# A pipelined kernel of four graph layers: the loop over passes written out, two biases added on VectorE, the scores spread with one fp32 matmul, other orders

## The chip, the cores and the metric

One core of a Trainium2 chip. The metric is the device time of one execution in microseconds: the median of several runs. A core has TensorE (PE in the profile; its weight loads are PEld), VectorE (DVE), ScalarE (ACT), GpSimd (POOL) and SyncE (SP), each with an instruction queue of its own that runs strictly in the order written, and they meet only at semaphores.

## What is computed

The input is 128 small graphs: `x` (128 graphs, 128 nodes, 256 features) and a weighted adjacency matrix `adj` (128x128 for each graph). Each of four layers takes `h = max(layernorm(x), 0)` and adds its own result to `x`:

```
L0  hypergraph convolution: with H = (adj != 0) and degrees from H and adj's first row,
    twice  out = Dn * (H @ (Be * (H^T @ (x @ W^T)))) + b, with relu and a layernorm between
L1  tanh(norm(adj) @ h @ W + b)
L2  s = h @ w @ a;  A = exp(leaky(8*tanh((s_i + s_j)/8))) * adj, rows rescaled;  A @ h @ w
L3  three times  adj @ (h @ W) + b, with relu after the first and the second
```

Everything is in float32. The kernel must keep near to fp32 precision, which shapes the way it multiplies.

## The kernel before

**Tiling.** Two graphs (J = 2) are worked on together as one unit, with the 128 nodes on the partitions. Four such units, the streams A to D, are in flight at a time, a quarter of a period apart; 16 passes of four streams make the 128 graphs. This text calls the work of one stream in one pass a turn: there are 64 turns, and in the steady state PE works in each turn on parts of all four streams.

**Steps.** A turn has seven products by a matrix of graph size (steps 0U to 6U) and seven by weights (0W to 6W). A U step is four fp32 matmuls of 128 columns into a PSUM bank (1U: eight). ScalarE then copies the bank into an fp32r tile UHI (`take`, L442), VectorE writes the rest, bank minus UHI, into ULO (`low`, L590), and the W step (`weigh`, L346) multiplies in three parts, UHI by WLO, UHI by WHI and ULO by WHI, as fp32r matmuls of 256 columns (512 for 0W). WHI and WLO are the weights split in the same way in the start. The trace records an fp32 matmul as two rows, an fp32r matmul as one.

**Biases of 4W and 5W.** The first matmul of these two steps (L357, L358) multiplies a constant tile SHARES by BIAS, 128x512 in fp32r, which puts the bias into the bank. BIAS holds the fp32r half of the bias on 64 partitions and the remainder on the others; it is made in the start by four casts (L535) and four subtractions (L541). When the step has ended, ScalarE takes the relu straight from the bank (`relu`, L483) and frees it; the next U step (5U or 6U) waits for this relu.

**Scores.** In layer L2 VectorE sums the score of each node (2N, L629). Two small operations split it, a cast SHI (2H, L637) and a difference SLO (2L, L641). PE spreads the scores over the columns (3S, `spread_scores`, L379) with four fp32r matmuls of 128 columns, each with one column of scores as stationary operand, repeated 128 times, and the identity as moving one. ScalarE's tanh and two exps, and VectorE's 3L and 3R, follow; `sums_done` at the end of 3R frees that bank.

**Banks.** U steps other than 1U, W steps other than 0W, G and 3S share four single banks in turn, so each waits for the fourth user before it to be released (`bank_free`, L292); 0W and 1U share two double banks.

**Order.** What each engine does next is written out by hand. Five tables of slots (L20 to L37) give each step of stream A a time within a period of 88; stream B's are 22 later, and so on. `ordered` (L40) sorts them. The slots do nothing but give the order in which each engine's instructions are written. `run` (L162) writes the pass 0, then a hardware loop (`Fori`, L173) over passes 1 to 15, whose waits compare with register values, then what is left of the last pass. SyncE has its own loop (L265).

Of the kernel before, what the change touches and what calls it, by code (L numbers as in the profile page):

```python
# [37 lines left out]


def ordered(slots):  # L40

# [8 lines left out]
PE_ORDER, ACT_ORDER, DVE_ORDER, POOL_ORDER, SP_ORDER = map(ordered, (PE_SLOTS, ACT_SLOTS, DVE_SLOTS, POOL_SLOTS, SP_SLOTS))  # L50


def program(nc, xs, adj_t, adj_r, w1t, w2t, l1w, l2w, l2wt, l3w1, l3w2, l3w3, cols, b1, b2, l1b, l3b1, l3b2, l3b3, out):
# [6 lines left out]
    with ExitStack() as ctx:  # L60
# [76 lines left out]
        WIDE_TURNS = [x for x in PE_ORDER if x[1] in WIDE_STEPS]  # L137
        BANK_TURNS = [x for x in PE_ORDER if x[1] not in WIDE_STEPS]

        def bank(s, step):  # L140
            turns, banks = (WIDE_TURNS, WIDE) if step in WIDE_STEPS else (BANK_TURNS, BANK)
            return banks[[x[:2] for x in turns].index((s, step)) % len(banks)]

        SETUP = WIDE[1 - [x[:2] for x in WIDE_TURNS].index(("A", "0W")) % 2]

# [14 lines left out]
        LIVE = [(s, back) for s in STREAMS for back in (0, -1)]  # L160

        def run(eng, order, parts, setup={}, per_pass=(1,)):  # L162

            def values(k):
                return {(s, back): dict(dma=16 * (k + back + 1), v=[J * done_at(s, k + back) - J + j + 1 for j in range(J)],
                                        **{f"n{m}": m * done_at(s, k + back) for m in per_pass}) for s, back in LIVE}

            for s, step, back in order:
                if not back:
                    parts[step](s, values(0)[s, 0], 0)  # L170
                    if (s, step) in setup:
                        setup[s, step]()
            with eng.Fori(1, GROUPS) as k:  # L173
                loop = {(s, back): {f"n{m}": eng.snap(len(STREAMS) * m * k + m * done_at(s, back)) for m in per_pass}
                        for s, back in LIVE}
                dma = {back: eng.snap(16 * k + 16 * (back + 1)) for back in (0, -1)}
                for s, back in LIVE:
                    loop[s, back]["dma"] = dma[back]
                    loop[s, back]["v"] = [eng.snap(len(STREAMS) * J * k + J * done_at(s, back) - J + j + 1) for j in range(J)]
                for s, step, back in order:  # L180
                    parts[step](s, loop[s, back], loop)
            for s, step, back in order:
                if back:
                    parts[step](s, values(GROUPS)[s, back], GROUPS)

        @block.sync
        def _(sp):
# [65 lines left out]
            def one_pass(k):  # L253
                for s, step, back in SP_ORDER:
                    if isinstance(k, int) and not (0 if step == "O" else 1) <= k + back < GROUPS:
                        continue
# [16 lines left out]
        def _(pe):  # L273
# [18 lines left out]
            def bank_free(s, step, k):  # L292
# [543 lines left out]
```

## Time and profile before

| | |
|---|---|
| median of 3 runs | 1413.41 us (1413.35 to 1413.74) |
| the profiled execution, its own time | 1413.38 us |
| its span in the trace | 1411.6 us (1.8 us lie around it) |
| TensorE busy | 1373.7 us, 97% |
| VectorE busy | 1168.9 us, 83% |
| ScalarE busy | 999.3 us, 71% |
| GpSimd busy | 998.7 us, 71% |

How to read it: a busy time is the union of the times of an engine's instructions. Matmuls overlap in the records, so what one costs is read as the distance between the starts of two that follow each other, in the timeline, not as its recorded length. Instructions that only wait, branch or set registers are not counted as busy. In rows that name a group, x is how many records it has.

### The profile page before, as it was taken

Reading aid. Unit: us, or ns where it says so; the run is one execution under the profiler, and the core shown is the slowest. Engines: PE = TensorE matmul, PEld = TensorE weight load, DVE = VectorE, ACT = ScalarE, POOL = GpSimd, SP = SyncE. Lnnn points to the kernel's source line nnn. Section 1 sums busy time; section 2 is a strip of 40 time slices with the busy share of each in tenths; the row PEclk is TensorE's granted clock in tenths of the full one; section 3 lists DMA queues with packets and bytes.
Section 4 is the critical chain, followed back from the end, with each engine's and each line's share of the span. In section 5 each row is a group of like instructions: output and inputs, shape, how many; then the busy total and the mean of one; then the engine's idle time right before and its main releaser. Section 6 shows DMA issues by size and latency. Waiting matters only on the chain.

```text
span 1411.6 us, 34650 instructions
## 1 busy us (share of the span) xinstructions
PE 1373.7 (97%) x10900; PEld 1325.3 (94%) x10900; DVE 1168.9 (83%) x3873; ACT 999.3 (71%) x2376; POOL 998.7 (71%) x2005
## 2 busy tenths in 40 slices
PE   4899999999999999999999999999999999999997
PEld 3799999999999999999999999999999999999996
DVE  5788888888888888888888888888888888888874
ACT  3577777777777777777777777777777777777763
POOL 3677777777777777777777777777777777777751
PEclk8999999999999999999999999999999999999999
DMA  7011120110110110110110110121211111111100
GB/s 190 1 42 28 53 52 26 52 52 26 52 52 26 52 52 26 52 52 26 52 52 26 52 52 27 52 52 28 50 52 29 49 52 29 49 52 32 31 20 23
DMA packets 83080, 62.70 MB, mean 44 GB/s; under 512 B 40305, under 2 KB 65521, under 8 KB 83057
## 3 DMA queue, kind: packets, MB, share of 16 engines
q1 hardware_dynamic: 83056, 62.43, 16.2%
q8 instruction: 11, 0.18, 0.1%
q14 instruction: 13, 0.10, 0.0%
HBM read 45.62 MB, written 16.78 MB: 44 GB/s over the span
## 4 chain that ended last, share of the span: by engine, by line
PE 95%; DVE 2%; POOL 1%; ACT 1%; issue 0%; DMA 0%; SPq 0%; DVEq 0%; POOLq 0%; ACTq 0%
PE BANK L366 29%; PE BANK L331 24%; PE BANK L373 15%; PE WIDE L366 8%; PE WIDE L342 8%; PE WIDE L373 4%; PE BANK L358 2%; PE BANK L316 2%; PE BANK L385 2%; DMA W<-in_w1t 0%; PE WIDE L279 0%; DVE BN_A L552 0%; POOL LN_A L730 0%; DVE WLO1W L502 0%; DVE BN_C L552 0%
## 5 line engine op out<-in xcount | busy, mean ns | idle before, releaser
L445 ACT ACTIVATE UHI_B<-BANK 128x512 fp32r<-128x512 f32 x96 | 57.3, 597 | 45.1 <-PE BANK L331 45.1
L445 ACT ACTIVATE UHI_C<-BANK 128x512 fp32r<-128x512 f32 x96 | 57.2, 596 | 42.2 <-PE BANK L331 42.2
L445 ACT ACTIVATE UHI_D<-BANK 128x512 fp32r<-128x512 f32 x96 | 57.2, 596 | 41.0 <-PE BANK L331 41.0
L445 ACT ACTIVATE UHI_A<-BANK 128x512 fp32r<-128x512 f32 x96 | 57.2, 596 | 40.2 <-PE BANK L331 40.2
L593 DVE TENSOR_TENSOR ULO_D<-BANK,UHI_D 128x512 fp32r<-128x512 f32 x96 | 65.9, 686 | 23.1 <-ACT UHI_D L445 22.4
L593 DVE TENSOR_TENSOR ULO_C<-BANK,UHI_C 128x512 fp32r<-128x512 f32 x96 | 65.9, 686 | 17.2 <-ACT UHI_C L445 16.5
L593 DVE TENSOR_TENSOR ULO_A<-BANK,UHI_A 128x512 fp32r<-128x512 f32 x96 | 65.9, 687 | 15.3 <-ACT UHI_A L445 15.0
L593 DVE TENSOR_TENSOR ULO_B<-BANK,UHI_B 128x512 fp32r<-128x512 f32 x96 | 65.8, 686 | 13.6 <-ACT UHI_B L445 12.9
L726 POOL TENSOR_TENSOR LN_D<-MV_D,EPS 128x2 f32<-128x2 f32 x80 | 15.7, 196 | 75.9 <-DVE MV_D L560 75.9
L726 POOL TENSOR_TENSOR LN_A<-MV_A,EPS 128x2 f32<-128x2 f32 x80 | 15.8, 197 | 73.1 <-DVE MV_A L560 73.1
L726 POOL TENSOR_TENSOR LN_B<-MV_B,EPS 128x2 f32<-128x2 f32 x80 | 15.9, 198 | 64.3 <-DVE MV_B L560 64.3
L726 POOL TENSOR_TENSOR LN_C<-MV_C,EPS 128x2 f32<-128x2 f32 x80 | 15.7, 196 | 61.9 <-DVE MV_C L560 61.8
L730 POOL TENSOR_TENSOR LN_B<-LN_B,MHALF 128x2 f32<-128x2 f32 x80 | 55.9, 699 | 1.3
L730 POOL TENSOR_TENSOR LN_D<-LN_D,MHALF 128x2 f32<-128x2 f32 x80 | 55.8, 697 | 1.3
L730 POOL TENSOR_TENSOR LN_A<-LN_A,MHALF 128x2 f32<-128x2 f32 x80 | 55.7, 697 | 1.3
L730 POOL TENSOR_TENSOR LN_C<-LN_C,MHALF 128x2 f32<-128x2 f32 x80 | 55.7, 696 | 1.3
L414 ACT ACTIVATE H_A<-RES_A,LN_A 128x256 f32<-128x256 f32 x96 | 52.2, 594 | 2.0 <-POOL LN_A L738 2.0
L331 PE MATMUL BANK<-T_D,H_D 128*128 128x128 f32 x384 | 52.0, 278 | 1.6 <-ACT H_D L486 1.4
L414 ACT ACTIVATE H_D<-RES_D,LN_D 128x256 f32<-128x256 f32 x96 | 52.2, 594 | 1.9 <-POOL LN_D L738 1.9
L414 ACT ACTIVATE H_C<-RES_C,LN_C 128x256 f32<-128x256 f32 x96 | 52.2, 594 | 0.9 <-POOL LN_C L738 0.9
L331 PE MATMUL BANK<-T_C,H_C 128*128 128x128 f32 x384 | 51.9, 278 | 0.9 <-ACT H_C L486 0.7
L414 ACT ACTIVATE H_B<-RES_B,LN_B 128x256 f32<-128x256 f32 x96 | 52.2, 595 | 0.5 <-POOL LN_B L738 0.5
(508 smaller groups left out, 5920.1 us busy)
## 6 DMA issues: line engine op xcount, KB each, us to landing
X_A<-in_xs SPq DMA_DIRECT2D x16, 256.0 KB, 2.8
X_B<-in_xs SPq DMA_DIRECT2D x16, 256.0 KB, 2.8
X_C<-in_xs SPq DMA_DIRECT2D x16, 256.0 KB, 2.8
X_D<-in_xs SPq DMA_DIRECT2D x16, 256.0 KB, 2.8
out_rows<-O_A SPq DMA_DIRECT2D x16, 256.0 KB, 2.0
out_rows<-O_B SPq DMA_DIRECT2D x16, 256.0 KB, 2.1
out_rows<-O_C SPq DMA_DIRECT2D x16, 256.0 KB, 2.1
out_rows<-O_D SPq DMA_DIRECT2D x16, 256.0 KB, 2.1
```

What stands on the lines that cost most here:

```text
L316: last = nc.tensor.matmul(bank(s, "G")[:, j * (P + 2):(j + 1) * (P + 2)], HT[s][:, j, :], BHT[s][:, j, :], start=True, stop=True)
L331: last = nc.tensor.matmul(bank(s, step)[:, at:at + P], lhs[s][:, j, m * P:(m + 1) * P], rhs(s, j), start=True, stop=True)
L342: last = nc.tensor.matmul(bank(s, "1U")[:, j, m * P:(m + 1) * P], Z[s][:, j, m * P:(m + 1) * P], GZ[s][:, j, :], start=True, stop=True)
L358: nc.tensor.matmul(to[:, :], SHARES[:, :], BIAS[step][:, :, :], start=True, stop=False)
L366: nc.tensor.matmul(dst, UHI[s][:, at[m]:at[m] + P], w[:, m, :], start=(w is lo and m == 0 and not biased), stop=False)
L373: last = nc.tensor.matmul(dst, ULO[s][:, at[m]:at[m] + P], hi[:, m, :], start=False, stop=(m == chunks - 1 and (j == J - 1 or not biased)))
L385: last = nc.tensor.matmul(bank(s, "3S")[:, j * P:(j + 1) * P], part[s][:, j:j + 1].to_broadcast([P, P]), IDENTR[:, :], start=(part is SHI) ...
L414: nc.scalar.activation(dst[s][:, j, :], src[s][:, j, :], ACT.Relu, bias=LN[s][:, NB, j:j + 1], scale=LN[s][:, RSTD, j:j + 1]).then_inc(sem ...
L445: nc.scalar.activation(UHI[s][:, 0:J * D], bank(s, step)[:, :], ACT.Copy).then_inc(sem(f"c{step}"), 1)
L593: nc.vector.tensor_tensor(ULO[s][:, 0:J * D], bank(s, step)[:, :], UHI[s][:, 0:J * D].bitcast(F32), ALU.subtract).then_inc(sem(f"l{step}"), 1)
L726: nc.gpsimd.tensor_tensor(ve, MV[s][:, :, 1], EPS[:, :], ALU.add).then_inc(sem("ve" + tag), 1)
L730: nc.gpsimd.tensor_tensor(rstd, ve, MHALF[:, :], ALU.pow)\
```

## The change

- The hardware loops are gone: every engine's 16 passes are written out one after the other, and each wait has a constant. The rotation of the banks is worked out over all passes.
- 4W and 5W have no bias matmul. A new VectorE step of each name adds the bias row to the bank (128x512, `b4W`, `b5W`) and writes H; ScalarE's relu then waits for that step, reads H and writes H. The bank is released by VectorE's step. BIAS, SHARES and their eight operations in the start are gone.
- 3S has two fp32 matmuls, straight from the scores and the identity, in the place of four fp32r ones. VectorE's 2H and 2L are gone, with the tiles SHI, SLO and IDENTR.
- All five slot tables have other values. In a turn PE's order was 5U 3U 2W 5W G 3W 1U 6U 1W 6W 0U 4U 3S 0W 4W 2U. It is now 5U 2U 3U 5W 2W 3W G 6U 1U 6W 1W 4U 0U 3S 4W 0W (each step of whichever stream is due). On VectorE 4W now stands right ahead of 3L, 3R and 3E, and 5W behind 2U, 0A and 3U.

```diff
 PE_SLOTS = {
-    "G": 5.35, "0U": 12.31, "0W": 15.06, "1U": 28.24, "1W": 29.30, "2U": 37.53, "2W": 47.58, "3S": 58.05,
-    "3U": 67.04, "3W": 71.77, "4U": 79.22, "4W": 81.45, "5U": 88.19, "5W": 92.43, "6U": 94.56, "6W": 97.75}
+    "G": 5.03, "0U": 18.28, "0W": 23.04, "1U": 29.55, "1W": 34.98, "2U": 45.66, "2W": 48.39, "3S": 63.29,
+    "3U": 68.21, "3W": 70.61, "4U": 83.87, "4W": 86.20, "5U": 89.28, "5W": 91.09, "6U": 93.96, "6W": 100.54}
...
 DVE_SLOTS = {
+    "T": 3.90, "X": 4.63, "XA": 14.25, "DA": 18.63, "DB": 18.99, "DC": 20.57, "DD": 30.10, "0U": 32.13,
+    "0W": 35.26, "0S": 36.47, "0A": 37.90, "1U": 42.66, "1W": 49.42, "1S": 50.94, "1A": 52.77, "2U": 59.47,
+    "2W": 61.69, "2S": 64.38, "2A": 64.62, "2N": 71.31, "3L": 77.37, "3R": 78.92, "3E": 79.04, "3U": 82.01,
+    "3I": 83.33, "3J": 84.12, "3W": 84.15, "3S": 84.54, "3A": 84.64, "4U": 94.08, "4W": 98.78, "5U": 102.44,
+    "5W": 104.12, "6U": 107.62, "6W": 109.61}
...
-        def run(eng, order, parts, setup={}, per_pass=(1,)):
...
-            with eng.Fori(1, GROUPS) as k:
...
+        def run(slots, parts, setup={}, per_pass=(1,)):
+
+            for s, step, k in ordered(slots, GROUPS):
+                parts[step](s, passed(s, k, per_pass), k)
+                if not k and (s, step) in setup:
+                    setup[s, step]()
...
-                    if biased:
-                        nc.tensor.matmul(to[:, :], SHARES[:, :], BIAS[step][:, :, :], start=True, stop=False)
...
-                pe.wait_ge(sem("scores_split"), c["n1"])
+                pe.wait_ge(sem("s_ready"), c["n1"])
                 bank_free(s, "3S", k)
                 for j in range(J):
-                    for part in (SHI, SLO):
-                        last = nc.tensor.matmul(bank(s, "3S")[:, j * P:(j + 1) * P], part[s][:, j:j + 1].to_broadcast([P, P]),
-                                                IDENTR[:, :], start=(part is SHI), stop=(part is SLO))
+                    last = nc.tensor.matmul(bank(s, "3S", k)[:, j * P:(j + 1) * P], ST[s][:, SC, j:j + 1].to_broadcast([P, P]),
+                                            IDENT[:, :], start=True, stop=True)
...
             def relu(step):
                 def f(s, c, k):
-                    act.wait_ge(sem(f"p{step}"), c["n1"])
-                    nc.scalar.activation(H[s][:, :, :], bank(s, step)[:, :], ACT.Relu).then_inc(sem(f"c{step}"), 1)
+                    act.wait_ge(sem(f"b{step}"), c["n1"])
+                    nc.scalar.activation(H[s][:, :, :], H[s][:, :, :], ACT.Relu).then_inc(sem(f"c{step}"), 1)
...
+            def biased(step):
+                def f(s, c, k):
+                    dve.wait_ge(sem(f"p{step}"), c["n1"])
+                    rows = bank(s, step, k)[:, :].rearrange("p (j d) -> p j d", j=J)
+                    nc.vector.tensor_tensor(H[s][:, :, :], rows, pair(BIAS[step][:, :]), ALU.add).then_inc(sem(f"b{step}"), 1)
```

## Rows read from the trace of the kernel before

**Rows 1.** The page: busy times, granted clock, the chain by engine.

```profile
PE 1373.7 (97%) x10900; PEld 1325.3 (94%) x10900; DVE 1168.9 (83%) x3873; ACT 999.3 (71%) x2376; POOL 998.7 (71%) x2005
...
PEclk8999999999999999999999999999999999999999
...
PE 95%; DVE 2%; POOL 1%; ACT 1%; issue 0%; DMA 0%; SPq 0%; DVEq 0%; POOLq 0%; ACTq 0%
```

**Rows 2.** Busy times from 76 to 1357 us, then in two stretches of one loop turn.

```profile
core 0: us, PE busy (x) PEld busy (x) DVE busy (x) ACT busy (x) POOL busy (x), PEclk, DMA share, GB/s
...
76.00:1357.00 1281.00, 1280.96 (x10286) 1242.17 (x10285) 1089.68 (x3627) 938.22 (x2243) 940.82 (x1874) 1.00 0.15 42
...
97.00:181.60 84.60, 84.60 (x682) 82.07 (x681) 72.01 (x241) 61.95 (x148) 62.19 (x124) 1.00 0.17 45
520.00:604.60 84.60, 84.60 (x682) 82.07 (x681) 72.04 (x241) 61.96 (x148) 62.20 (x124) 1.00 0.15 43
```

**Rows 3.** A wait of PE in the start: us in total, times, longest.

```profile
PE WIDE L342 <- ACT GZ_A L461: 4.0, 1, 4.0
```

**Rows 4.** Timeline of PE, one stream's turn: start, us, then the group.

```profile
700.00 0.39 PE L358 MATMUL BANK<-BIAS5W,SHARES 128*128 128x512 f32 x1
700.23 0.40 PE L366 MATMUL BANK<-WLO5W,UHI_B 128*128 128x256 f32 x2
700.46 0.40 PE L366 MATMUL BANK<-WHI5W,UHI_B 128*128 128x256 f32 x2
...
702.01 0.49 PE L366 MATMUL BANK<-WLO3W,UHI_C 128*128 128x256 f32 x2
702.33 0.39 PE L366 MATMUL BANK<-WHI3W,UHI_C 128*128 128x256 f32 x2
...
703.47 1.95 PE L342 MATMUL WIDE<-GZ_A,Z_A 128*128 128x128 f32 x16
705.25 1.06 PE L331 MATMUL BANK<-T_B,H_B 128*128 128x128 f32 x8
...
711.28 1.06 PE L331 MATMUL BANK<-T_C,H_C 128*128 128x128 f32 x8
712.10 0.30 PE L385 MATMUL BANK<-IDENTR,SHI_D 128*128 128x128 f32 x1
...
712.58 0.68 PE L366 MATMUL WIDE<-WLO0W,UHI_B 128*128 128x512 f32 x2
...
721.15 0.39 PE L358 MATMUL BANK<-BIAS5W,SHARES 128*128 128x512 f32 x1
```

**Rows 5.** DVE and ACT groups of stream A, by form.

```profile
L593 DVE TENSOR_TENSOR ULO_A<-BANK,UHI_A 128x512 fp32r<-128x512 f32 x96 | 65.9, 687 | 15.3 <-ACT UHI_A L445 15.0
...
L639 DVE CAST SHI_A<-ST_A 128x2 fp32r<-128x2 f32 x16 | 11.5, 719 | 0.6
...
L643 DVE TENSOR_TENSOR SLO_A<-ST_A,SHI_A 128x2 fp32r<-128x2 f32 x16 | 2.4, 149 | 0.0
...
L486 ACT ACTIVATE H_A<-BANK 128x512 f32<-128x512 f32 x32 | 18.9, 591 | 12.3 <-PE BANK L373 12.3
```

**Rows 6.** The larger instruction queue, q8: 50 to 176 us, then 176 to 1360 us.

```profile
q8 instruction: 7, 0.11, 0.4%
...
q8 instruction: 1, 0.02, 0.0%
```

**Rows 7.** Timeline of the start: DVE, then PE.

```profile
26.88 0.48 DVE L535 CAST BIAS4W<-L3B 128x256 fp32r<-128x256 f32 x2
...
29.25 0.69 DVE L502 TENSOR_TENSOR WLO2W<-O_A,WHI2W 128x512 fp32r<-128x512 f32 x1
...
34.03 3.78 PE L342 MATMUL WIDE<-GZ_A,Z_A 128*128 128x128 f32 x16 [4.04 <-ACT GZ_A L461]
```

**Rows 8.** Timeline of the end, stream D alone: PE and ACT.

```profile
1399.33 0.60 ACT L486 ACTIVATE H_D<-BANK 128x512 f32<-128x512 f32 x1 [2.01 <-PE BANK L373]
...
1399.98 1.16 PE L331 MATMUL BANK<-T_D,H_D 128*128 128x128 f32 x8 [0.69 <-ACT H_D L486]
```

More of the change, by code:

```diff
@@ L82, in program @@
         B2, L1B, L3B1, L3B2, L3B3 = (sb(n, [P, D]) for n in ("B2", "L1B", "L3B1", "L3B2", "L3B3"))
-        BIAS = {step: sb(f"BIAS{step}", [P, J, D], F32R) for step in ("4W", "5W")}
-        SHARES = sb("SHARES", [P, P], F32R)
+        BIAS = {"4W": L3B1, "5W": L3B2}
         BW = sb("BW", [P, D])
@@ L89, in program @@
         IDENT = sb("IDENT", [P, P])
-        IDENTR = sb("IDENTR", [P, P], F32R)
         OFFDIAG = sb("OFFDIAG", [P, P])
@@ L136, in program, with banks_for, bank @@
         WIDE_STEPS = ("0W", "1U")
[L137 to L144, printed above, removed]
+        def banks_for(step):
+            return WIDE if step in WIDE_STEPS else BANK
+        TURN, LAST_USER, users = {}, {}, {True: [], False: []}
+        for user in ordered(PE_SLOTS, GROUPS):
+            alike, banks = users[user[1] in WIDE_STEPS], banks_for(user[1])
+            TURN[user] = len(alike) % len(banks)
+            if len(alike) >= len(banks):
+                LAST_USER[user] = alike[-len(banks)]
+            alike.append(user)
+        def bank(s, step, k):
+            return banks_for(step)[TURN[s, step, k]]
+        SETUP = WIDE[1 - TURN["A", "0W", 0]]
         W1, W2, W2G = sb("W1", [P, DC, DH]), sb("W2", [P, HC, D]), sb("W2G", [P, HC, D])
@@ L158, in done_at, with passed @@
             return len(STREAMS) * k + STREAMS.index(s) + 1
-        LIVE = [(s, back) for s in STREAMS for back in (0, -1)]
-        def run(eng, order, parts, setup={}, per_pass=(1,)):
[L164 to L172, printed above, removed]
-            with eng.Fori(1, GROUPS) as k:
[L174 to L184, printed above, removed]
+        def passed(s, k, per_pass=(1,)):
+            return dict(dma=16 * (k + 1), v=[J * done_at(s, k) - J + j + 1 for j in range(J)],
+                        **{f"n{m}": m * done_at(s, k) for m in per_pass})
+        def run(slots, parts, setup={}, per_pass=(1,)):
[3 more added lines that the diff above has]
+                    setup[s, step]()
         @block.sync
@@ L251, in _ @@
             parts = {"X": load_x, "F": load_front, "W": load_first_row, "D": load_diagonal, "R": load_r, "T": load_t, "O": store}
[L253 to L256, printed above, removed]
-                    before = back if step == "O" else back - 1
-                    n = len(STREAMS) * k + done_at(s, before)
-                    if isinstance(k, int):
-                        parts[step](s, k + back, n)
-                    else:
-                        parts[step](s, k + back, sp.snap(n))
-            one_pass(0)
-            with sp.Fori(1, GROUPS - 1) as k:
-                one_pass(k)
-            one_pass(GROUPS - 1)
-            one_pass(GROUPS)
+            for s, step, k in ordered(SP_SLOTS, GROUPS):
+                if k or step == "O":
+                    parts[step](s, k, done_at(s, k if step == "O" else k - 1))
             for s in STREAMS:
@@ L330, in f @@
                             at = j * D + m * P
-                            last = nc.tensor.matmul(bank(s, step)[:, at:at + P], lhs[s][:, j, m * P:(m + 1) * P], rhs(s, j),
+                            last = nc.tensor.matmul(bank(s, step, k)[:, at:at + P], lhs[s][:, j, m * P:(m + 1) * P], rhs(s, j),
                                                     start=True, stop=True)
@@ L366, in f @@
                                 nc.tensor.matmul(dst, UHI[s][:, at[m]:at[m] + P], w[:, m, :],
-                                                 start=(w is lo and m == 0 and not biased), stop=False)
+                                                 start=(w is lo and m == 0), stop=False)
                         if step == "1W":
```

112 lines of the change are left out of this document (38 added, 74 removed), and 11 rows, old and new, of tables (ACT_SLOTS, DVE_SLOTS).

## The prediction

> **What bounds the kernel now.** I read the page first: PE is busy for 97% of the span, its granted clock is full in all slices but the first, where it is 0.8, and the chain that ended last is PE for 95% [rows 1]. A busy PE need not be a full one, so I asked next for windows. From 76 to 1357 us PE is busy for 1280.96 of 1281.00 us [rows 2]: it waits for nothing. Two bias matmuls of the same step, one turn apart,, the first and the last row of [rows 4], start 21.15 us from each other, and 64 turns of that are 1354 us; the rest is the filling and emptying of the pipeline. In those 1281 us (60.6 turns) DVE is busy for 1089.7 us and ACT for 938.2 [rows 2], so 18.0 and 15.5 us of each turn. In the steady state only PE's own work counts; what the others do costs nothing while it comes in time. The reader should take from this that two questions decide: how much PE work goes, and whether PE still never waits.
>
> All sums are against the profiled execution, 1413.38 us (span 1411.6 and 1.8 around it); the median is 1413.41, so the two can be taken as one.
>
> **Bias matmuls.** The one of 5W starts at 700.00 and the next matmul at 700.23 [rows 4], so it holds PE for 0.23 us. There are two in each turn, 128 in all: 128 x 0.23 = **29.4 us less**. The Trainium skill (TensorE: Matmul & The Clock Gate, Back-to-back issue gap) states a sustained spacing of 131 ns for matmuls of 512 columns, and by that only 16.8 us would go. The trace has 230 ns for this one in its place, and the sum goes by it.
>
> **Scores.** Four fp32r matmuls from 712.10 to 712.58 take 0.48 us [rows 4]. The two fp32 matmuls in their place are four records of the kind of 1U, whose 16 records take 705.25 - 703.47 = 1.78 us, 0.111 each, so 0.445. A change from fp32 to fp32r costs something as well: the first WLO3W pair behind G takes 0.32 us where a pair of 5W takes 0.23 [rows 4]. The old order has four blocks of fp32 in a turn, the last of them leading into the cheap fp32r 3S; the new one has three. That would be 0.035 + 0.04 us less, 5 us in all. Against it: a T unit inside a block takes 0.82 us (711.28 to 712.10), 0.103 for a record, when it is followed by today's 3S, and the same eight records at 1U's 0.111 take 0.89; with 3S in fp32 this shorter unit may go. That is 0.07 us a turn, 5 us more. Stationary operands read with a repeat of one column are fp32r here, in fp32 no row shows them; between those ends I take **0**, range -5 to +5.
>
> **DVE.** It gains two adds of 128x512 from PSUM, like the ULO operation at 0.687 us, and loses the cast at 0.719 and the difference at 0.149 [rows 5]: 18.0 + 1.37 - 0.87 = 18.5 us in a turn. PE's new turn is 21.15 - 0.46 = 20.69, so DVE is at 89%, from 85%. ACT's relu (0.591 [rows 5]) stays, now with its input in SBUF: 15.5 of 20.7, 75%. GpSimd does the same as before. Their load costs **0**; what hides it is 2.2 us of free DVE time in a turn, down from 3.1, and the order has to keep each result in time.
>
> **The added step on the path.** 5U waits for 4W's relu and 6U for 5W's. In the end, where nothing hides it, relu starts at 1399.33 and 5U at 1399.98 [rows 8], 0.65 us; the add ahead of it is about 0.69 + 0.04, so the way from the end of a W step to its U step becomes some 1.42 us. What covers it in the steady state: behind 4W comes 0W, 12 matmuls of 512 at about 0.23, 2.8 us. Behind 5W come 2W and 3W (six pairs of 0.23 each) and G (four fp32 records of 0.111), 3.2 us. So 1.4 and 1.8 us are left for operations that stand ahead in DVE's and ACT's queues. Followed through one turn, DVE has 2U's ULO, a small aggregate and 3U's ULO in front of 5W's add (1.5 us), but these can start before 5W has ended, and I find 6U served about 0.4 us early. 2U's normalised input, 1U's scaled G (behind 5W's relu on ACT) and 6W's ULO come out 0.3 to 0.5 us early too. The margins are thin and all on the right side. The banks: the add releases 4W's, which 5W needs next, behind 0W, 5U, 2U and 3U, some 5.5 us; 5W's goes to 6U, which waits for 5W's relu in any case. Bank of 3S: 3U is still the fourth user, with 0W, 4W, 5U and 2U between (about 6 us, as before). Steady state: **0**.
>
> **Loops written out.** Each wait on a register becomes one on a constant, and no engine branches. PE is busy for 84.60 of 84.60 us in the stretch from 97 us and again in the one from 520 [rows 2]. Both hold a turn of the loop or its seam, so the branch cost PE no idle time; 0.04 us a pass, one unit of what I can read, is the most: **0.6 us less**. The price is more code to fetch. Queue q8 brought seven packets from 50 to 176 us and one from 176 to 1360 [rows 6]: the loop's code stayed where it was. Now the fetching of the first stretch goes on all the time, and in the first stretch PE was as full as later. Cost **0**. The Trainium skill (Runtime: NRT & Kernel Launch, Instruction fetch mechanics) has a taken branch wait for a fetch when its target is not in a small window; by that each of 14 turns back would have cost a fetch. The rows show no such gap.
>
> **Start.** The eight bias operations on DVE, from 26.88 to 29.25 us [rows 7], stand ahead of the aggregate that leads to GZ_A, for which PE waits 4.0 us at 34.03 [rows 3, 7]. With them gone that wait is **2.4 us** shorter. The first pass is otherwise in PE's old order. **End.** With one or two streams left the added step is bare: 4W to 5U for B, C and D, and 5W to 6U for D, 0.73 us each: **3 us more**.
>
> Sum: 1413.4 - 29.4 + 0 - 0.6 - 2.4 + 3.0 = **1384.0 us**, 2.1% less. What a measurement can tell from no change is about 0.2%, 2.8 us.
>
> **The rivals.**
> - *A partial stall (15%).* One of the thin margins is negative and PE waits some 0.3 us in each turn: 64 x 0.3 = 19, **1403 us**. For it: DVE at 89% with strict order, four margins of 0.3 to 0.5 us. Against: the load leaves 2.2 us.
> - *The add is late (7%), slower than before.* 5W's add stands behind an operation of DVE that itself waits for ACT (the statistics of 0W need its relu, in front of 2U's ULO), so that 6U waits for the add and one more operation: 0.69 + 0.59 = 1.3 us beyond the cover in each turn, minus the 0.46 gained: 64 x 0.8 = 54, **1467 us**. It decides from the point where PE waits over 0.46 us in a turn. Against it: the wait must outlast 3.2 us of PE work.
> - *Matmuls of another pace (8%).* The same matmuls stand at 0.22 to 0.24 us a pair here. If new neighbours bring the 30 pairs of a turn nearer to the low end, by 0.005 each, that is 0.15 x 64 = 10 us less: **1374 us**.
> - *The bias matmul was cheap (4%).* It hides loading that now shows between its neighbours, as much as behind G, 0.32 - 0.23 = 0.09 us [rows 4]: 1384 + 128 x 0.09 = **1396 us**. Nothing else in the rows speaks for it. The spacing that the Trainium skill states (TensorE: Matmul & The Clock Gate, Back-to-back issue gap) would come out on this side.
> - *The spread in fp32 is dear (2%).* If a repeated column loads slowly, say each record at the double 0.22: 64 x 0.44 = 28, **1412 us**, no change.
>
> **How the numbers follow.** The forecast has 64%; its own range is the bounds of the score term and of start and end, 1378 to 1391. The range reaches from the paces' gain to the partial stall: 1375 to 1403. Faster by over 0.2%: forecast, partial stall, pace and cheap bias, 64 + 15 + 8 + 4, less one for the stall's own tail, 90%. Within 0.2%: 3%, the dear spread and that tail. Slower: 7%.
>
> **What would show it.** Right: PE's idle time in the middle stays near 0, the distance between turns is 20.6 to 20.8 us, 5W's last matmul is followed by 2W, DVE is busy near 89%, q8 has packets throughout, GZ_A's wait is near 1.6 us. Wrong: waits of PE for H by ACT's relu, or for a ULO, in every turn; records of 3S far from 0.11 us apart; gaps of PE that nothing ends, at the rhythm of the fetches; a clock below full in the middle.

## The result, and the profile after

| | before | after |
|---|---|---|
| median of 4 runs | 1413.57 us (1413.35 to 1413.74) | 1376.43 us (1374.89 to 1377.13) |
| ratio | | 0.9733 [0.9721, 0.9745] |
| the profiled execution | 1413.38 us, span 1411.6 | 1375.74 us, span 1374.0 |

The kernel is 2.7% faster; 1384.0 us had been forecast, with 1375 to 1403 around it. The direction and the main mechanism (the bias matmuls leave a PE that never waits) held. The measured time lies 1.4 us inside the lower end of the range and outside the forecast's own 1378 to 1391. The gain is 37 us where 29.4 had been expected, and the difference has two sides: a gain that I had only as a rival (the pace of the matmuls that stay), less a loss that I had not seen at all (VectorE's products beside GpSimd).

The page of the kernel after: busy times, granted clock, queue q8, the chain by engine.

```profile
PE 1334.7 (97%) x10772; PEld 1289.6 (94%) x10772; DVE 1238.5 (90%) x3863; ACT 1000.8 (73%) x2376; POOL 996.9 (73%) x2005
...
PEclk8999999999999999999999999999999999999999
...
q8 instruction: 88, 1.44, 0.4%
...
PE 93%; DVE 2%; POOL 1%; ACT 1%; SPq 1%; issue 1%; DMA 1%; DVEq 0%; POOLq 0%
```

Against [rows 1], PE has 128 matmuls less and 39 us less, DVE 70 us more with ten instructions less. The windows of after answer to [rows 2] (busy PE, PEld, DVE, ACT, POOL, then clock and DMA share):

```profile
0.00:76.00 76.00, 51.90 (x311) 45.59 (x312) 51.03 (x165) 39.82 (x90) 45.30 (x100) 0.91 0.38 101
76.00:1320.00 1244.00, 1243.99 (x10190) 1209.53 (x10189) 1158.49 (x3629) 939.88 (x2243) 937.85 (x1877) 1.00 0.16 45
1320.00:1374.00 54.00, 38.81 (x275) 34.48 (x273) 28.95 (x72) 21.06 (x44) 13.74 (x30) 0.96 0.06 20
```

PE is still full in the middle. DVE is at 93% there, not at the 89% of the prediction.

**Where the 37.6 us of span went.** Take the first and the 60th matmul group of step 5W in either trace. Before:

```profile
86.45 0.39 PE L358 MATMUL BANK<-BIAS5W,SHARES 128*128 128x512 f32 x1
...
1334.74 0.39 PE L358 MATMUL BANK<-BIAS5W,SHARES 128*128 128x512 f32 x1
```

After:

```profile
81.51 0.48 PE L323 MATMUL BANK<-WLO5W,UHI_A 128*128 128x256 f32 x2
...
1291.41 0.48 PE L323 MATMUL BANK<-WLO5W,UHI_D 128*128 128x256 f32 x2
```

So the start is 4.9 us shorter, the 59 turns between are 1248.3 - 1209.9 = 38.4 us shorter, and the end (76.9, then 82.6 us) is 5.7 us longer. Start and end together lose 0.8 us; the gain is all in the steady state, where a turn (one stream's work in one pass) went from 21.16 to 20.51 us.

**What is in a turn.** The timeline of PE, in the kernel after, around one 5W:

```profile
614.14 1.06 PE L291 MATMUL BANK<-AE_D,H_D 128*128 128x128 f32 x8
614.96 0.48 PE L323 MATMUL BANK<-WLO5W,UHI_C 128*128 128x256 f32 x2
615.28 0.39 PE L323 MATMUL BANK<-WHI5W,UHI_C 128*128 128x256 f32 x2
615.50 0.39 PE L330 MATMUL BANK<-WHI5W,ULO_C 128*128 128x256 f32 x2
615.73 0.39 PE L323 MATMUL BANK<-WLO5W,UHI_C 128*128 128x256 f32 x2
...
616.18 0.39 PE L330 MATMUL BANK<-WHI5W,ULO_C 128*128 128x256 f32 x2
616.41 0.39 PE L323 MATMUL BANK<-WLO2W,UHI_A 128*128 128x256 f32 x2
```

From 615.28 to 616.18 eight matmuls start in 0.90 us, 113 ns each. In the kernel before, the pairs of 5W stood 0.23 to 0.24 us apart. I worked the spacing out in this way for every whole block of twelve matmuls of 256 columns (24 in 1W) between 76 and 1320 us: start of the sixth group less start of the second, over the matmuls between. The means of some 50 to 60 blocks each, in ns, for all kernels that the text needs:

| kernel | 1W | 2W | 3W | 4W | 5W | 6W |
|---|---|---|---|---|---|---|
| before | 117.7 | 113.9 | 113.9 | 115.5 | 117.9 | 117.8 |
| after | 113.5 | 113.5 | 113.5 | 119.2 | 113.5 | 115.7 |
| loop written out only (e1) | 117.8 | 116.5 | 114.9 | 115.6 | 117.8 | 117.8 |
| after, both bias matmuls (e5) | 113.3 | 117.9 | 117.8 | 117.7 | 117.7 | 113.8 |
| after, one bias matmul, 4W (e11) | 113.3 | 113.3 | 113.3 | 117.5 | 113.5 | 115.7 |
| after, one bias matmul, 5W (e12) | 113.3 | 113.9 | 113.9 | 118.4 | 113.9 | 115.4 |
| after, X3 later (e7) | 113.4 | 113.4 | 113.3 | 117.6 | 113.3 | 115.5 |
| e7 with 0U behind 3S (e10) | 113.4 | 114.5 | 114.5 | 117.7 | 114.5 | 115.2 |

The distance between two matmuls has one of two values, about 113.5 or about 118 ns. Most blocks keep one of them, but not all. In 6W of the new kernel the pace changes in the middle of the block, in 58 of 61 blocks: two distances of a pair at 0.24 us, then 0.22 and 0.23.

```profile
622.49 0.40 PE L323 MATMUL BANK<-WHI6W,UHI_C 128*128 128x256 f32 x2
622.73 0.39 PE L330 MATMUL BANK<-WHI6W,ULO_C 128*128 128x256 f32 x2
622.97 0.39 PE L323 MATMUL BANK<-WLO6W,UHI_C 128*128 128x256 f32 x2
623.19 0.39 PE L323 MATMUL BANK<-WHI6W,UHI_C 128*128 128x256 f32 x2
623.42 0.39 PE L330 MATMUL BANK<-WHI6W,ULO_C 128*128 128x256 f32 x2
```

4W of the kernel before does the same in all of its 59 blocks, so its 115.5 ns is a change inside each block and not a mixture of blocks. And W blocks that follow each other with no fp32 work between them keep the pace with which the block ahead ended: behind 6W comes 1W, behind 5W come 2W and 3W, and in the new kernel these follow it in every turn, narrow in 58 or 59 of them and wide in two.

In the new kernel 1W, 5W and a part of 6W went from the wide spacing to the narrow one, and 4W the other way. By the table that is 24 x 4.2 + 12 x (0.4 + 0.4 - 3.7 + 4.4 + 2.1) = 144 ns in a turn. (4W's 119.2 lies above both spacings, since 12 of its 60 blocks hold a wait of some 0.06 us for their low half. Without these waits, as in e7, it is at 117.6, and the pace alone is worth 0.16 us.) With the two bias matmuls (0.23 + 0.23) the 144 ns explain 0.60 of the 0.65 us. The last 0.05 is the balance of 3S (0.48, now 0.40), of one entry less from fp32 into fp32r (0.32 for the first pair, not 0.23) and of fp32 units, some of which take 0.89 where they took 0.81.

**What had not been expected: 2N.** DVE's groups of stream A in the kernel after, by form; 2N and the added addition, which has no row in [rows 5] but was costed by them.

```profile
L585 DVE SCALAR_TENSOR_TENSOR Z_A<-H_A,WA 128x256 f32<-128x256 f32 x32 | 26.7, 867 | 0.0
...
L577 DVE TENSOR_TENSOR H_A<-BANK,L3B 128x512 f32<-128x512 f32 x32 | 21.7, 679 | 0.0
```

The group of 2N in the kernel before:

```profile
L633 DVE SCALAR_TENSOR_TENSOR Z_A<-H_A,WA 128x256 f32<-128x256 f32 x32 | 13.7, 449 | 0.4 <-ACT H_A L414 0.4
```

The added addition costs 0.68 us, as forecast. But 2N, the two products that give the scores, has doubled in its mean, from 0.45 to 0.87 us, with no change of its own. The timeline of DVE and GpSimd at one of them:

```profile
297.39 1.29 POOL L732 TENSOR_TENSOR RES_D<-RES_D,L3B 128x512 f32<-128x512 f32 x1
298.63 0.89 POOL L700 TENSOR_TENSOR ST_B<-ST_B,MHALF 128x2 f32<-128x2 f32 x1
...
297.60 1.36 DVE L585 SCALAR_TENSOR_TENSOR Z_A<-H_A,WA 128x256 f32<-128x256 f32 x1
298.89 0.08 DVE L585 DVE_READ_ACCUMULATOR Z_A<-H_A,WA 128x1 f32 x1
298.89 0.42 DVE L585 SCALAR_TENSOR_TENSOR Z_A<-H_A,WA 128x256 f32<-128x256 f32 x1
...
299.24 0.87 DVE L561 SCALAR_TENSOR_TENSOR RES_B<-BANK,ST_B,RES_B 128x256 f32<-128x256 f32 x2
```

The first product starts 0.2 us behind GpSimd's X3 (L732) and ends 0.3 us behind it; the second, with X3 over, takes 0.42. It is as if the first had stood still for most of X3. This is so in nearly every turn: between 76 and 1320 us the median of the first product is 1.36 us, that of the second 0.41. The Trainium skill (SBUF — State Buffer, "SBUF: two separate sides") has a rule for this: DVE's operation with two SBUF inputs and a GpSimd operation that reads SBUF share one pair of ports as an exclusive lock, and whichever starts second is blocked for the other's whole length. The rows agree for X3: 1.36 us beside it, 0.42 without. They don't agree for every GpSimd operation. The second product begins at 298.89, inside L700 (two columns of SBUF, from 298.63 to 299.52 by the records), and still takes 0.42, in all of the 59 turns in which the two meet in this way. So here only the addition of 128x512 blocked, and what sets its reach is not shown. The addition of the biases reads one input from PSUM and stays at 0.68.

Whom does it delay? Behind 2N in DVE's queue stands 1W of the next stream (L561), ended at 300.1 here. PE:

```profile
298.81 1.06 PE L291 MATMUL BANK<-G_C,H_C 128*128 128x128 f32 x8
299.70 0.61 PE L341 MATMUL BANK<-IDENT,ST_A 128*128 128x128 f32 x4
300.25 0.47 PE L323 MATMUL BANK<-WLO4W,UHI_D 128*128 128x256 f32 x2
```

From 3S to 4W it is 0.55 us here, in most turns 0.37. Nine of 48 turns between 200 and 1200 us are so, by up to 0.26. In all nine 4W starts 0.15 us behind the end of that operation of DVE, in most others about 0.25 us behind it, which speaks for 4W having waited for this bank. No row calls it a wait, since the end of a matmul in the records is a model and covers the gap: the distance of the starts shows what the busy time of 1243.99 in 1244.00 us does not.

The collision comes in nearly every turn, the late 3S in nine. What picks them out is, for six of them at least, a second and smaller thing. The late ones recur every 16 turns, and ahead of six of the nine DVE has 0.3 to 0.4 us more idle time than in other turns. Ahead of the one above:

```profile
292.95 0.25 DVE L505 BATCH_NORM_AGGREGATE MV_D<-BN_D 128x2 f32<-128x6 f32 x2 [0.33 <-issue]
```

"issue" means that nothing in the profile ended this idle time. In the kernel before no idle time of DVE between 200 and 1200 us is over 0.2 us longer than the usual one at its place. With nothing but the loop written out (e1), one at 300.8 us is 0.36 longer, and so are those at 639.8 and 978.7, again 16 turns apart; there they delay nothing on PE. So these stops came with the written-out code. That they are its fetching is likely, but no run shows it.

**Start and end.** The waits of PE in the kernel after (engine, tile, line, releaser: us in total, times, longest); the first answers to [rows 3]:

```profile
PE WIDE L302 <- ACT GZ_A L417: 2.0, 1, 2.0
...
PE BANK L341 <- DVE Z_D L585: 1.6, 1, 1.6
```

And the end of the timeline of PE, against [rows 8]:

```profile
1361.63 1.16 PE L291 MATMUL BANK<-T_D,H_D 128*128 128x128 f32 x8 [1.45 <-ACT H_D L442]
...
1366.85 1.16 PE L291 MATMUL BANK<-T_D,H_D 128*128 128x128 f32 x8 [1.45 <-ACT H_D L442]
```

A bare step from W to U now has 1.45 us of idle time where it had 0.69: 0.76 for the add, as worked out (0.73). It is bare four times (4W of B, C and D, 5W of D), and for B no part of it was bare before: the kernel before has three such waits there.

### The profile page after: what moved, and what is told of

Its sections match the earlier page's. It is cut to its first block, busy times and chain, and to the rows that moved or that the text cites. A ratio compares the mean times of both kernels' runs of the same rounds, so it can differ in the third digit from the quotient of the medians.

```text
span 1374.0 us, 32347 instructions
## 1 busy us (share of the span) xinstructions
PE 1334.7 (97%) x10772; PEld 1289.6 (94%) x10772; DVE 1238.5 (90%) x3863; ACT 1000.8 (73%) x2376; POOL 996.9 (73%) x2005
## 4 chain that ended last, share of the span: by engine, by line
PE 93%; DVE 2%; POOL 1%; ACT 1%; SPq 1%; issue 1%; DMA 1%; DVEq 0%; POOLq 0%
PE BANK L323 30%; PE BANK L291 24%; PE BANK L330 15%; PE WIDE L323 8%; PE WIDE L302 8%; PE WIDE L330 4%; PE BANK L341 2%; PE BANK L276 2%; DMA X_B<-in_xs 1%; SPq L226 0%; DVE BN_C L497 0%; ACT H_D L370 0%; DVE BN_B L497 0%; DVE Z_B L585 0%; ACT UHI_D L401 0%
## 5 line engine op out<-in xcount | busy, mean ns | idle before, releaser
L291 PE MATMUL BANK<-T_B,H_B 128*128 128x128 f32 x384 | 51.3, 277 | 1.4 <-ACT H_B L442 1.4
L291 PEld LDWEIGHTS BANK<-T_D,H_D 128*128 128x128 f32 x384 | 47.8, 191 | 5.0 <-ACT H_D L442 3.3
L291 PEld LDWEIGHTS BANK<-T_C,H_C 128*128 128x128 f32 x384 | 47.8, 191 | 3.7 <-ACT H_C L442 1.9
L291 PEld LDWEIGHTS BANK<-T_B,H_B 128*128 128x128 f32 x384 | 48.3, 193 | 3.0 <-ACT H_B L442 1.6
```

The source lines that it names most:

```text
L291: last = nc.tensor.matmul(bank(s, step, k)[:, at:at + P], lhs[s][:, j, m * P:(m + 1) * P], rhs(s, j), start=True, stop=True)
```

## The experiments

Each kernel ran beside runs of the kernel before on the same chip; the ratio is to those.

**e1_written_out.** The kernel after with the old slot tables, the bias matmuls and the fp32r scores back, so that the loop written out is all that is left of the change.

```diff
-            with eng.Fori(1, GROUPS) as k:
...
+            for s, step, k in ordered(slots, GROUPS):
```

> The kernel before with its passes written out and nothing else changed: old slot tables, bias matmuls on PE, four fp32r matmuls for the scores. Theory A (the extra gain beyond my sum comes from PE's order, which decides at which of two spacings, 113.5 or 117.7 ns, a block of 256-column matmuls runs): PE's turn stays 21.15 us, 1W, 6W and 5W stay at 117.7 ns, time 1412 to 1414 us. Theory B (waits on registers and the loop slowed PE's issue): the turn falls by 0.15 us or so, 1403 us, and 1W goes to 113.5 ns.

Measured: 1413.18 us, 0.9993 [0.9983, 1.0002]. The turn is 21.18 us, against 21.16. Queue q8 brings 77 packets between 176 and 1360 us, where it was one [rows 6], and PE is full. Alone, writing out brings nothing and costs nothing that the time shows; neither its gain of 0.6 us nor a price of fetching can be seen in it. 1W, 5W and 6W stay at 117.8 ns, so the loop is not what made them wide. DVE's three stops are new, as said above.

**e2_dve_biases.** e1 without the bias matmuls, with the adds on VectorE in the old order.

```diff
-DVE_SLOTS = {
+DVE_SLOTS = {"4W": 91.5, "5W": 97.5,
...
-                        nc.tensor.matmul(to[:, :], SHARES[:, :], BIAS[step][:, :, :], start=True, stop=False)
...
+                    nc.vector.tensor_tensor(H[s][:, :, :], rows, pair(BIAS[step][:, :]), ALU.add).then_inc(sem(f"b{step}"), 1)
```

> e1 with the biases of 4W and 5W added on VectorE (its two steps put at 91.5 and 97.5 in the old table), nothing else. By my sum 29.4 us less for the matmuls, 2.4 less in the start, 3 more in the end: 1384 us if e1 is 1413, and with a turn of 20.69. Theory A: that, with 1W and 6W still at 117.7 ns; 5W may change its spacing, since it follows 2W now and not a bias matmul, 3 us either way. Theory C (the bias matmul slows its neighbours and the removal itself gives the extra gain): 1376 us or less, 1W and 6W at 113.5. Rival for the order: VectorE's old order is not made for the two adds, so PE waits in each turn, 1390 to 1410.

Measured: 1618.31 us, 1.1449 [1.1430, 1.1468]; the turn is 24.34 us. The waits of PE between 200 and 1200 us:

```profile
PE BANK L294 <- ACT H_B L446: 33.8, 22, 1.7
PE BANK L294 <- ACT H_D L446: 31.4, 20, 1.7
PE BANK L294 <- ACT H_C L446: 30.7, 20, 1.7
PE BANK L294 <- ACT H_A L446: 30.7, 20, 1.7
```

H by ACT's relu (L446): 5U waits for 4W's, 6U for 5W's. Each is waited for up to 1.7 us, since the adds stand too late in DVE's queue and PE's old order has too little between W and U. They sum to 126.6 us in 41 turns, 3.1 us in each. Neither the 1384 us nor the 1390 to 1410 of the expectation came. This is the rival of the late add, at more than twice the 1.3 us that I had given it, in the old order.

**e3_fp32_scores.** e1 with the scores spread in fp32, and 2H and 2L gone.

```diff
-    "2U": 47.94, "2W": 50.48, "2S": 51.69, "2A": 52.99, "2N": 56.85, "2H": 56.91, "2L": 59.70, "3L": 66.92,
+    "2U": 47.94, "2W": 50.48, "2S": 51.69, "2A": 52.99, "2N": 56.85, "3L": 66.92,
```

> e1 with the scores spread by two fp32 matmuls and without the cast and the difference on VectorE, nothing else. My sum gave 0, range -5 to +5, against e1: 1408 to 1418. Theory A: the blocks behind 3S (0W, 4W) may change their spacing, all others stay. Theory D (the fp32 spread gives the extra gain): 1403 us.

Measured: 1412.65 us, 0.9991 [0.9981, 1.0001]. From 3S to the next step it is 0.37 us, not 0.48; the T unit ahead of it went from 0.81 to 0.89 and 0W from 2.85 to 2.89. The two sides of my term of 0 are both there, with their sizes (0.11, and 0.08 + 0.04), and cancel.

**e4_after_old_orders.** All of the change but the slot tables, with the adds at e2's places.

```diff
 PE_SLOTS = {
-    "G": 5.03, "0U": 18.28, "0W": 23.04, "1U": 29.55, "1W": 34.98, "2U": 45.66, "2W": 48.39, "3S": 63.29,
+    "G": 5.35, "0U": 12.31, "0W": 15.06, "1U": 28.24, "1W": 29.30, "2U": 37.53, "2W": 47.58, "3S": 58.05,
...
```

> The changed kernel with the old slot tables on all engines (VectorE's 4W and 5W put at 91.5 and 97.5, without 2H and 2L). Theory A: the extra gain is lost, 1W and 6W at 117.7 ns, turn 20.65 to 20.75, 1384 to 1388 us. If parts other than the order made the gain: 1374 to 1378 us.

Measured: 1619.95 us, 1.1462 [1.1443, 1.1481]. The same as e2, and far from the 1384 to 1388 expected. With the old orders and the adds at these places the change is a loss of 15%.

**e5_after_pe_bias.** The kernel after with both biases back on PE, its orders kept.

```diff
-    "3I": 83.33, "3J": 84.12, "3W": 84.15, "3S": 84.54, "3A": 84.64, "4U": 94.08, "4W": 98.78, "5U": 102.44,
-    "5W": 104.12, "6U": 107.62, "6W": 109.61}
+    "3I": 83.33, "3J": 84.12, "3W": 84.15, "3S": 84.54, "3A": 84.64, "4U": 94.08, "5U": 102.44,
+    "6U": 107.62, "6W": 109.61}
...
+                    biased = step in BIAS
+                    if biased:
+                        nc.tensor.matmul(to[:, :], SHARES[:, :], BIAS[step][:, :, :], start=True, stop=False)
```

> The changed kernel with the two bias matmuls back on PE and relu from the bank, new orders otherwise. Theory A: 128 x 0.23 = 29.4 us more, 3 us less in the end and 2.4 more in the start: 1405 us, 1W and 6W still at 113.5 ns; 2W and 3W, which would follow a bias matmul's block, may go to 117.7, 5 us more. Theory C (the bias matmul itself slows the neighbours): 1413 us or more, 1W and 6W at 117.7 too.

Measured: 1408.55 us, 0.9971 [0.9961, 0.9981]: 32.1 us above the kernel after, though 29 us of matmuls came back. In the table 2W, 3W and 5W are now wide: 36 matmuls x 4.4 ns = 0.16 us in a turn. The wait for GZ_A is back at 4.04 us, and the first 5W at 83.87: the start term is shown, 2.0 us of wait and 2.4 us at 5W (0.2 of it is the bias matmul of the 4W ahead). All the new orders by themselves, against e3, are worth 3 to 4 us (0.9971 against 0.9991, and the two intervals touch).

**e6_after_fp32r_scores.** The kernel after with cast and difference (2H, 2L) and four fp32r matmuls in 3S.

```diff
-DVE_SLOTS = {
+DVE_SLOTS = {"2H": 71.4, "2L": 71.6,
...
+                    for part in (SHI, SLO):
```

> The changed kernel with the four fp32r matmuls for the scores, the cast and the difference back (VectorE's 2H and 2L right behind 2N). My price: 0, range -5 to +5 against the changed kernel. The cast took 0.72 us of VectorE before, so VectorE is at 97% and 3S comes later by 0.9 us: since 3S already is PE's only late step (up to 0.24 us late in a quarter of the turns), PE waits 0.5 to 0.9 us in each turn, 1405 to 1430 us. If VectorE's load is not what makes 3S late: 1371 to 1381 us.

Measured: 1410.88 us, 0.9986 [0.9976, 0.9995]. The waits of PE, again from 200 to 1200 us:

```profile
PE BANK L345 <- DVE SLO_D L600: 4.3, 12, 1.1
PE BANK L345 <- DVE SLO_A L600: 4.0, 12, 0.6
PE BANK L345 <- DVE SLO_C L600: 3.8, 12, 0.7
PE BANK L345 <- DVE SLO_B L600: 3.4, 12, 0.3
```

Every 3S waits for the low half of the scores, about 0.3 us by the records and 0.48 by the starts (0U to 3S is 1.38 us, in the kernel after 0.89): 64 x 0.48 = 31 of the 34.5 us. So in the new order the scores' part is worth 34.5 us, where alone (e3) it was worth nothing: the way from the scores to 3S had no slack left for two more DVE operations at this place. Other places for them were not tried.

**e7_x3_later.** The kernel after with one slot changed: GpSimd's X3 no longer meets 2N.

```diff
-    "N1": 41.34, "2A": 49.38, "N2": 50.94, "2S": 60.59, "N3": 72.68, "X3": 79.13}
+    "N1": 41.34, "2A": 49.38, "N2": 50.94, "2S": 60.59, "N3": 72.68, "X3": 85.50}
```

> The changed kernel with one slot changed: GpSimd's last bias (X3) moves from 79.13 to 85.50, behind the two operations of N1 and in front of RX, away from VectorE's 2N. Theory E (2N's product of two SBUF tensors stands still while GpSimd's tensor_tensor runs: 1.36 us at 605.23, until GpSimd's ends at 606.30): 2N falls from a mean of 867 to about 450 ns, VectorE from 93% to 89%, the 0.24 us waits of 3S go, turn 20.44 throughout, 3 to 5 us less: 1371 to 1373 us. Rival: 2N is slow for another reason or the waits come from elsewhere: 1375 to 1377 us.

Measured: 1371.44 us (1370.49 to 1373.59), 0.9712 [0.9699, 0.9726], the best of all. By the medians it is 5.0 us below the kernel after, by the ratios 3.0, by the spans of the two profiled executions 4.3. DVE's group in e7:

```profile
L585 DVE SCALAR_TENSOR_TENSOR Z_A<-H_A,WA 128x256 f32<-128x256 f32 x32 | 12.4, 424 | 0.0
```

Two pieces of it in the timeline of DVE:

```profile
603.61 0.41 DVE L585 SCALAR_TENSOR_TENSOR Z_D<-H_D,WA 128x256 f32<-128x256 f32 x1
...
603.94 0.42 DVE L585 SCALAR_TENSOR_TENSOR Z_D<-H_D,WA 128x256 f32<-128x256 f32 x1
```

And the window:

```profile
76.00:1320.00 1244.00, 1244.00 (x10221) 1211.39 (x10220) 1113.88 (x3637) 942.29 (x2248) 932.16 (x1883) 1.00 0.16 45
```

2N is back at 0.42 us, DVE at 89.5%, every turn takes 20.45 us and every 3S 0.37. Without the collision no turn is late, though DVE's three stops without a cause are still there (292.5, 619.7 and 946.8 us): the collision had used up the slack that they needed. That the turns came late by way of 1W's bank is read from the timeline, and no run holds that way apart from the others.

**e8_early_adds.** e2 with the adds placed earlier on DVE, as early as their matmuls allow.

```diff
-DVE_SLOTS = {"4W": 91.5, "5W": 97.5,
+DVE_SLOTS = {"4W": 90.81, "5W": 94.7,
```

> e2 with VectorE's two adds put as early as the old order allows: 4W behind 3E (90.81), 5W behind 3U (94.70). In e2 PE waits about 1.9 us for 4W's relu (4W to the unit after 2U took 2.78 us where 0.89 is its work) and 1.5 us for 5W's. Theory F (PE's old order has only 2U, 0.89 us, between 4W and 5U, and add and relu take 1.42, so no place on VectorE can hide them): PE still waits 0.5 to 1.3 us in each turn, 1415 to 1470 us. Rival (my place for the adds alone made e2 slow): 1384 to 1390 us.

Measured: 1439.24 us, 1.0185 [1.0168, 1.0202]. 6U no longer waits. 5U still does, for up to 0.6 us and in every turn:

```profile
PE BANK L294 <- ACT H_A L446: 6.6, 12, 0.6
```

Between 4W and 5U PE's old order has only 2U. A better DVE order saves most of the 205 us of e2. By these waits, what is left needs more of PE's work between 4W and 5U, and the new order puts 0W there; no run moved 0W alone.

**e9_t_before_1w.** e7 with 6U behind 1U and 6W behind 1W in PE's order, to see if the spacing of 6W and 1W goes by what stands ahead of them.

```diff
-    "3U": 68.21, "3W": 70.61, "4U": 83.87, "4W": 86.20, "5U": 89.28, "5W": 91.09, "6U": 93.96, "6W": 100.54}
+    "3U": 68.21, "3W": 70.61, "4U": 83.87, "4W": 86.20, "5U": 89.28, "5W": 91.09, "6U": 95.60, "6W": 101.10}
```

> e7 with PE's 6U behind 1U and 1W in front of 6W, as in the old order (6U at 95.60, 6W at 101.10). Theory A: 1W and 6W go to the wide spacing, 117.7 ns, since they follow the unit of T as before: 36 x 4.5 ns = 0.16 us a turn, 10 us more than e7, 1381 us, plus what PE waits for 1W's UHI and ULO, which now come right behind 6U (0 to 0.3 us a turn, to 1400 us). Rival (the spacing has to do with something other than what stands ahead of the block): 1W and 6W stay at 113 ns.

Measured: 1667.54 us, 1.1788 [1.1768, 1.1808]. PE's waits, 200 to 1200 us:

```profile
PE BANK L323 <- ACT UHI_C L407: 17.5, 10, 1.8
...
PE BANK L341 <- DVE RES_A L561: 17.3, 10, 1.7
```

1W now starts before its input is split, and 3S waits in turn for 1W's bank. The expectation had been 1381 to 1400 us. With such gaps the spacing says nothing: the question was not answered. What the run does show is the price of the order: two steps moved, 296 us. Not all of it is waiting, since the granted clock is 0.97 from 76 to 1500 us here, where it was 1.00.

**e10_0u_last.** e7 with 0U behind 3S, so that 4W follows 0U (and 2U stands ahead of 5W).

```diff
-    "G": 5.03, "0U": 18.28, "0W": 23.04, "1U": 29.55, "1W": 34.98, "2U": 45.66, "2W": 48.39, "3S": 63.29,
-    "3U": 68.21, "3W": 70.61, "4U": 83.87, "4W": 86.20, "5U": 89.28, "5W": 91.09, "6U": 93.96, "6W": 100.54}
+    "G": 5.03, "0U": 19.50, "0W": 23.04, "1U": 29.55, "1W": 34.98, "2U": 45.66, "2W": 48.39, "3S": 63.29,
+    "3U": 67.40, "3W": 70.61, "4U": 83.87, "4W": 86.20, "5U": 89.28, "5W": 91.09, "6U": 93.96, "6W": 100.54}
```

> e7 with 0U behind 3S and 3U in front of 2U, so that the two blocks of fp32 work end with other units (0U ahead of 4W, 2U ahead of 5W). Theory A: 4W, at 118 ns in all kernels where it follows the fp32 3S, goes to 113 ns behind 0U, 0.05 us a turn, 1368 us; the blocks behind 2U may stay at 113 ns or go to 118, 5W, 2W and 3W together 0.16 us a turn, 1378 us. If the unit ahead has no part: both stay as in e7, 1371 us. 3S and 3U come 0.9 us earlier, which costs waits if VectorE is not that much early.

Measured: 1374.78 us (1373.53 to 1375.51), 0.9730 [0.9714, 0.9746], 3 us above e7. 4W stays at 117.7 ns behind another unit: that the unit ahead decides its spacing falls. 5W, with 2U ahead of it now, is wide in 16 of 61 turns, 15 of them of stream B, and 2W and 3W are wide in the same ones.

**e11_pe_bias_4w_only** and **e12_pe_bias_5w_only.** e5 with the bias matmul for one of the steps alone, the other's bias being added on VectorE as in the kernel after (the diff is e11's).

```diff
-                    biased = step in BIAS
+                    biased = step == "4W"
...
+    "5W": 104.12, "6U": 107.62, "6W": 109.61}
```

> The changed kernel with the bias matmul back on PE for 4W alone (5W's stays on VectorE). Theory C2 (a bias matmul costs its own 0.22 us and, when it opens a block, the wide spacing in all W steps of that block): e5 had 118 ns in 5W, 2W and 3W, which follow 5W's bias matmul, and 0.22 us more in 4W, which is at 118 ns anyway. Here 5W, 2W, 3W stay at 113 ns and the turn grows by 0.22 us, 14 us more, 1391 us. If the two biases cost the same, half of 32: 1392 us.

> The changed kernel with the bias matmul back on PE for 5W alone. Theory C2: 5W, 2W and 3W at 118 ns, the turn grows by 0.27 + 0.05 + 0.05 = 0.37 us, 24 us more; less about 2 us for what the add costs in the end and what 3S waited: 1398 us. Rival (the spacing in e5 came from something else, such as VectorE's and ScalarE's lighter load or other addresses): 5W, 2W and 3W stay at 113 ns, 14 us more, 1390 us.

Measured: 1387.03 us, 0.9808 [0.9792, 0.9824], and 1387.75 us, 0.9811 [0.9795, 0.9827]. That is 10.6 and 11.3 us above the kernel after for 64 matmuls, 14.5 us at 0.226 each. The turn is 20.69 us in both, 0.19 more than in the kernel after. The bias matmul itself is there in full: from its start to the next fp32 unit 4W and 0W take 0.23 us more in e11, and 5W takes 0.22 more in e12. Some 0.03 us a turn comes back, since 3 of 49 turns have a late 3S in place of 9 of 48. That DVE has 64 adds less, and so more time, is the likely reason. e11 came 4 us below its 1391. In e12 the 1398 of theory C2 failed and the rival's 1390 was near: 2W, 3W and 5W are wide in only 8 of 60 turns, though the bias matmul stands right ahead of 5W, as in e5. The two extras sum to 21.9 us, and both together (e5) cost 32.1. Of the 10.2 us between, the wide blocks give the most: 5W, 2W and 3W together take 0.14 us a turn more in e5 than in e12, 9 us.

## Why the prediction was right, and where it was not

- **Bias matmuls, -29.4.** Right in kind and size. The turn lost 0.46 us for them, and e11 and e12 put them back one by one, at 0.23 and 0.22 us by the starts. The times of these two runs, 10.6 and 11.3 us above the kernel after, are less than 64 x 0.23 = 14.5, because start, end and late turns change with them. The figure of the Trainium skill that I had weighed against it (TensorE: Matmul & The Clock Gate, Back-to-back issue gap), 131 ns, would have given 16.8 us in all. The distances of 0.22 to 0.23 us in the traces are not near it.
- **The pace of the other matmuls.** This is the step that was off, a term put at nothing. The forecast kept their pace, and gave 8% to the rival that new neighbours bring them to the low end of 0.22 to 0.24 us a pair, for 0.15 us a turn and 10 us. That is what happened in size: 0.144 us by the table, 9.2 us over 64 turns. It did not come as an even shift of all pairs, but by whole runs of blocks that changed from one spacing to the other, 4W's against the rest. The rival's time was 1374, and the measured one is near it partly by luck: it also holds a longer end and the late turns, which no rival had. I had named the effect and its size from the rows, and its chance was my guess. The range began at 1375, a microsecond above this rival's own time. The trace of before would have borne more: 2W and 3W stood at the narrow spacing in most turns and 5W, 6W and 1W at the wide one in each, so the operation itself can do both.
- **Scores, 0.** In the old order exactly that (e3). In the new one the steady state has 0.05 us a turn left over for it and the late turns together, so it brought some 3 us net of them, within the -5 to +5. That "the cast and the difference go" is more than DVE's load I had missed: by e6, 34.5 us hang on it, with the two operations at the one place tried. The forecast is not hurt, as it asked only whether the new kernel waits, but the parts of this change have no prices of their own.
- **DVE, 18.5 us a turn.** With X3 out of the way it has 1113.88 us in 60.8 turns, 18.3. In the kernel after it has 1158.49 in 60.7, 19.1 us, for the 0.9 us that the first product of 2N takes longer. The sum counted operations at the durations that they had beside the old neighbours; a new order gives new neighbours. "GpSimd does the same as before" was true, and not enough.
- **The added step in the steady state, 0.** Right: the relus that 5U and 6U need are never waited for between 76 and 1320 us. The cover of 2.8 and 3.2 us against 1.42 was read off the new order, and e2 and e8 show what happens in the old one, where it was less. The rival of the partial stall (15%) came true in a small way, in another place: some 0.2 us in one turn of five, ahead of 4W, for 3 to 5 us (e7), not 19.
- **Loops, -0.6, and code, 0.** Nothing either way in the time of e1. With 14 turns back or none, it is the same, so the rule of the Trainium skill on fetching after a taken branch (Runtime: NRT & Kernel Launch, Instruction fetch mechanics) finds no gap to explain here. "Code, 0" held for PE alone: DVE's stops of 0.3 to 0.4 us are not in the kernel before but in e1 and in the kernel after, and with the collision beside them they go ahead of six of the nine late turns.
- **Start, -2.4.** GZ_A's wait is 2.0 us shorter, and e5 has the first 5W 2.4 us later. **End, +3.** Too small. The add is 0.76 us four times, and the margin that B's step had before (0.69) is gone as well, 3.7; 3S of D waits 1.6 us for 2N, which no row of before shows. That wait is 1.6 in e5 too, which has no added steps, so it comes with the new orders. From the 60th 5W on, the end is 5.7 us longer although it has matmuls less.
- **The sum.** In the 59 turns I had 59 x 0.46 + 0.6 = 27.7 us, and it was 38.4: 8.5 for the pace, 2.2 for scores and loops. In start and end I had a gain of 1.7 us (five turns' bias matmuls, 2.3, and -2.4 + 3.0) and it was a loss of 0.8. 1384.0 - 10.7 + 2.5 = 1375.8, and 1375.74 was measured; this closes because its terms are read from the same two traces, and is no test of them.

## What to carry to other kernels

Where one engine is full and never waits, the sum of what leaves it is a good forecast, but test the pace of what stays as well: start distances of like blocks, matmul by matmul, show whether they all run at their best. A change of order is also a change of who runs beside whom, so look through the new order for VectorE operations with two SBUF inputs beside GpSimd's long ones, and move one of them: a single slot gave 3 to 5 us here. And parts of such a change can't be priced alone: the adds cost 26 us without the new orders at the better of the two places tried for them, the scores brought 0 in the old order and 34.5 in the new, and only all of them together gave 37.

## What the hardware showed that I had not expected

- fp32r matmuls of 256 columns follow each other at one of two spacings, 113.5 or 118 ns, at full granted clock; W blocks in a row hand the spacing on, and inside a block it can change. It is not the loop (e1 keeps the wide ones), not the unit ahead alone (e10), not a bias matmul ahead (narrow in 52 of 60 turns in e12, wide in all in e5). Two more causes fall by the traces. It is not where the tiles lie: a stream's 5W uses the same tiles and the same bank in every pass, and in e12 each stream has it at both spacings, wide twice and narrow thirteen times. And the other engines are not needed for the wide one. At the end of the kernel after, stream D's last 5W is wide with nothing else at work (in the window's row, which has the columns of the windows above, DVE, ACT and POOL are the three 0.00 with (x0)):

```profile
1364.54 0.40 PE L323 MATMUL BANK<-WLO5W,UHI_D 128*128 128x256 f32 x2
1364.77 0.40 PE L323 MATMUL BANK<-WHI5W,UHI_D 128*128 128x256 f32 x2
1365.01 0.40 PE L330 MATMUL BANK<-WHI5W,ULO_D 128*128 128x256 f32 x2
...
1364.30:1365.30 1.00, 1.00 (x8) 0.90 (x8) 0.00 (x0) 0.00 (x0) 0.00 (x0) 1.00 0.00 0
```

  What chooses stays open.
- A VectorE product with two SBUF inputs took 1.36 us beside a GpSimd addition of 128x512 that had begun 0.2 us earlier, and 0.42 beside a GpSimd operation of 128x2 that had begun 0.3 us earlier.
- A fully busy PE in the records can hide 0.2 us of waiting in a turn.
